# A mixture-of-experts layer that computes only each token's two chosen experts, in sorted tiles of 128 rows

## The chip, the cores and the metric

The kernel runs on one core of a Trainium2 chip. The metric is the device time of one execution in microseconds (us), as the median of several runs. The engines are PE (TensorE, matrix products), DVE (VectorE), ACT (ScalarE), POOL (GpSimd) and SP (SyncE, which here only starts DMAs).

## What is computed

The input x has 16 batches of 128 time steps and 128 features, 2048 tokens in all. Layer 0 is a conditioned projection and a quantised gated feed-forward layer. Layer 1 is a recurrence over time, then a mixture of experts. Cut to what matters here:

```python
# layer 1, cond: a recurrence of 128 steps, on 16 batches at once
xw = x @ Wx + b
h[t] = tanh(xw[t] + h[t-1] @ Wh)
# layer 1, ffn: 8 experts, 128 -> 512 -> 128, two of them per token
logits = h @ router_w.T
values, chosen = top_k(logits, 2);  weight = softmax(values)
y[e] = gelu(h @ w1[e].T + b1[e]) @ w2[e].T + b2[e]
out = x + sum(weight[k] * y[chosen[k]] for k in (0, 1))
```

The reference computes all eight experts for each token and then takes two of them.

## The kernel before, in words

All of it is one program with an instruction stream for each engine. Tokens are in time-major order in the second layer: 16 batches of one time step are 16 neighbouring columns, and 8 steps are one tile of 128 tokens.

**Layer 0** (up to about 107 us) is a chain of products, quantisations by a global maximum, and rounding. DVE and ACT carry most of it. Meanwhile POOL (`split_weights`, L330) scales the expert weights, splits each of 16 chunks into a high and a low float16 part, and SP turns them with a transposing DMA (L275 to L280). The last two chunks are split by ACT (`weight_hi`, L403) and DVE (L701).

**The recurrence.** A step is one float32 matmul of 128x16 on PE (`first_step`, L911, and L985 to L988), which the trace shows as two weight loads and two matmuls, then a Tanh on ACT that writes the state into `h32` (L494, L517). PE's next step waits for that Tanh. The first 16 steps run beside the end of layer 0, the others in slots of the expert layer: `RNN_SLOTS` (L32) says in which of the eight slots of a pair of experts a step is issued.

**The expert layer** is dense. `WIDTHS` (L25) cuts the tokens into five chunks, whose states are complete in turn. `chunks` (L214) goes through the chunks and, in each, through four pairs of experts, three of these as a loop with the pair's number in a register. `pair` exists for PE (L967), ACT (L508) and DVE (L758). One slot is a quarter of one expert for all tokens of the chunk. In it PE makes the hidden product, three matmuls (high x high, low x high, high x low) over up to 512 columns, and the output product `down` (L956) of the slot four earlier, three matmuls of 128 columns for each tile. ACT takes the GELU (L523) and in some slots a second GELU in float16 (L525, `HI_SCALAR`). DVE makes the float16 high part (L789) and the low part (L793), and adds each expert's output, times the token's gate, to the accumulator (`add_gated`, L744). Each expert meets each token, whether it was chosen or not: the gate of one not chosen is zero.

**Routing** is done once for a chunk, in its first slots: logits by PE, top two by DVE (L711 to L742). POOL splits the states into float16 parts (L358), and multiplies the output biases by the gates and sums them (`sum_b2`, L365). SP stores each output tile when its chunk is complete (L282 to L290).

The order on every engine is written out by hand, and each wait is on a semaphore with a known count.

Of the kernel before, what the change touches and what calls it, by code (L numbers as in the profile page):

```python
# [5 lines left out]
F32, F16 = mybir.dt.float32, mybir.dt.float16  # L6
I8, U8 = mybir.dt.int8, mybir.dt.uint8
I16, U16 = mybir.dt.int16, mybir.dt.uint16
ALU = mybir.AluOpType
# [3 lines left out]
P = 128  # L13
# [18 lines left out]
RNN_SLOTS = ((0, 1, 3, 4, 5, 7), range(8), range(8), (0, 1, 2, 4, 5, 6), ())  # L32
RNN_FROM = [FIRST_STEPS + E // 2 * sum(len(n) for n in RNN_SLOTS[:c]) for c in range(CH)]
HI_SCALAR = ((3,), (), (3,), (3,), (0, 1, 3))
TS = P // B
SLOTS = E * NF
WS = 256.0
# [6 lines left out]
W_POOL = 14  # L44
# [4 lines left out]
W_CHUNKS = 2 * E  # L49


def program(nc, x, cond, w_cond, w_gate, w_up, w_down, w_x, w_h, b_h, w_router, w1, b1, w2, b2, out):
    ctx = ExitStack()
    with ctx:
# [6 lines left out]
        def sems(names):  # L61
# [5 lines left out]
        ident = sb("ident", [P, P])  # L67
        ident16 = sb("ident16", [P, P], F16)
# [30 lines left out]
        nat_wy = wyT[:, :, :].rearrange("p b o -> p (b o)").bitcast(F16).rearrange("p (a n) -> p a n", a=4)  # L99
        h32 = q[:, :, :].rearrange("p a n -> p (a n)").bitcast(F32)  # L100
# [6 lines left out]
        rw = sb("rw", [P, E])  # L107
        rw_hi = sb("rw_hi", [P, E], F16)
        rw_lo = sb("rw_lo", [P, E], F16)
        b2_all = sb("b2_all", [P, E, P])  # L110
# [4 lines left out]
        g32 = sig2[:, 0:NF * CT].rearrange("p (f n) -> p f n", f=NF)  # L115
        g_hi, g_lo = (sig2.bitcast(F16)[:, 2 * NF * CT * (i + 1):2 * NF * CT * (i + 2)].rearrange("p (a f n) -> p a f n", a=2, f=NF)
                      for i in range(2))
        h_hi, h_lo = (up2.bitcast(F16)[:, TOK * i:TOK * (i + 1)] for i in range(2))

        b2_prod = gate2[:, 0:E * P].rearrange("p (e n) -> p e n", e=E)  # L120
        b2_sum = gate2[:, E * P:E * P + 2 * CT].rearrange("p (a j n) -> p a j n", a=2, n=P)
        logit = sb("logit", [P, CTILES, E])
        top = sb("top", [P, CTILES, 8])
        topi = sb("topi", [P, CTILES, 8], U16)
        mixd = sb("mixd", [P, 4, CTILES])
        pick = sb("pick", [P, 2, CTILES, E])
        gates = sb("gates", [P, TOK // P, E])
# [3 lines left out]
        ld_cond, ld_gate, ld_up, ld_down, ld_misc, ld_wx, ld_b2 = sems(  # L131
# [20 lines left out]

        ps_rnn = banks[0]
        ps_y = [banks[1], banks[2]]
        ps_logits = banks[3]
        ps_h = banks[4:8]
        ps_pk = banks[7]
        Q_HI_SCALAR = (2, 3)
# [872 lines left out]
```

## Time and profile before

| | us |
|---|---|
| median of 3 runs | 349.01 |
| lowest and highest run | 348.28, 349.47 |
| the profiled execution, whole | 348.25 |
| its span, first to last instruction | 346.5 |
| end of the first 16 steps, start of step 16 | 107.3 |
| DVE busy | 315.1 (91%) |
| PE busy, matmuls | 265.4 (77%) |
| ACT busy | 213.1 (62%) |
| POOL busy | 158.3 (46%) |

The rows further down come from one profiled execution. A time at the start of a row counts from the span's start. PEld is PE's weight load, which runs beside its matmuls; SPq is the queue of DMAs that SP issues. Matmuls overlap, so that the sum of their durations is more than the time in which PE is busy. The arrow in brackets behind a row says how long the engine stood idle before it and who ended that idle time; "issue" means that it waited for nothing that the profile shows.

### The profile page before, as it was taken

Reading aid. Unit: us, or ns where it says so; the run is one execution under the profiler, and the core shown is the slowest. Engines: PE = TensorE matmul, PEld = TensorE weight load, DVE = VectorE, ACT = ScalarE, POOL = GpSimd, SP = SyncE. Lnnn points to the kernel's source line nnn. Section 1 sums busy time; section 2 is a strip of 40 time slices with the busy share of each in tenths; the row PEclk is TensorE's granted clock in tenths of the full one; section 3 lists DMA queues with packets and bytes.
Section 4 is the critical chain, followed back from the end, with each engine's and each line's share of the span. In section 5 each row is a group of like instructions: output and inputs, shape, how many; then the busy total and the mean of one; then the engine's idle time right before and its main releaser. Section 6 shows DMA issues by size and latency. Waiting matters only on the chain.

```text
span 346.5 us, 8439 instructions
## 1 busy us (share of the span) xinstructions
PE 265.4 (77%) x2601; PEld 190.9 (55%) x2601; DVE 315.1 (91%) x648; ACT 213.1 (62%) x427; POOL 158.3 (46%) x198
## 2 busy tenths in 40 slices
PE   5589330006698979997779999888999998776894
PEld 4434230002456867785557776556777666654673
DVE  4899999899996899799999899999889999999985
ACT  6289998160536765775447676555676665574692
POOL 1779994000086156016762109784111676639400
PEclk9989965556998998999999999999999999999999
DMA  7991443000015000000000000000001000001000
GB/s 204 332 282 38 97 86 61 0 0 0 0 33 121 2 0 0 3 2 18 0 0 0 2 23 4 0 0 0 2 0 32 0 1 0 2 3 31 0 2 23
DMA packets 28074, 12.13 MB, mean 35 GB/s; under 512 B 17369, under 2 KB 26898, under 8 KB 28050
## 3 DMA queue, kind: packets, MB, share of 16 engines
q1 hardware_dynamic: 27650, 11.63, 13.0%
q8 instruction: 13, 0.21, 0.2%
q10 hardware_dynamic: 400, 0.20, 0.2%
q14 instruction: 11, 0.09, 0.1%
HBM read 6.58 MB, written 1.05 MB: 22 GB/s over the span
## 4 chain that ended last, share of the span: by engine, by line
PE 39%; DVE 37%; issue 14%; POOL 3%; DVEq 2%; DMA 2%; ACT 2%; SPq 1%; ACTq 0%; POOLq 0%
PE bank L814 38%; DVE big L789 8%; DVE big L793 5%; DVE peak L562 5%; DVE wyT L749 5%; DVE big L658 2%; DVE big L668 2%; DMA x_sb<-in_x 2%; DVE big L641 2%; DVE peak L636 2%; DVE big L674 1%; DVE big L676 1%; POOL wnat L315 1%; POOL big L363 1%; ACT big L523 1%
## 5 line engine op out<-in xcount | busy, mean ns | idle before, releaser
L814 PE MATMUL bank<-wt,big 128*128 (+1 forms) x1536 | 116.3, 221 | 23.3 <-DVE big L793 14.6
L793 DVE TENSOR_TENSOR big<-big 128x384 f16<-128x384 f32 (+2 forms) x160 | 124.8, 787 | 9.5 <-ACT big L525 5.4
L814 PEld LDWEIGHTS bank<-wt,big 128*128 128x128 f16 x1536 | 97.6, 98 | 59.1 <-issue 36.2
L523 ACT ACTIVATE big<-bank,miscT 128x384 f32<-128x384 f32 (+2 forms) x160 | 96.3, 602 | 45.7 <-PE bank L814 41.3
L814 PE MATMUL bank<-big,wt 128*128 128x384 f16 (+2 forms) x480 | 110.3, 339 | 1.4 <-POOL big L363 1.4
L789 DVE CAST big<-big 128x512 f16<-128x512 f32 (+2 forms) x112 | 55.6, 497 | 7.2 <-ACT big L523 6.1
L361 POOL CAST big<-q 128x64 f16<-128x64 f32 x32 | 11.0, 344 | 98.1 <-ACT q L517 98.1
L517 ACT ACTIVATE q<-bank,miscT (+1 forms) x112 | 30.7, 274 | 39.7 <-PE bank L814 38.2
L814 PEld LDWEIGHTS bank<-big,wt 128*128 (+1 forms) x480 | 46.6, 117 | 13.7 <-POOL big L363 1.5
L814 PE MATMUL bank<-q,wxh 128*128 (+1 forms) x254 | 45.2, 254 | 2.1 <-ACT q L494 1.6
L814 PEld LDWEIGHTS bank<-q,wxh 128*128 128x128 f32 x254 | 39.1, 194 | 7.5 <-ACT q L494 3.7
L749 DVE SCALAR_TENSOR_TENSOR wyT<-bank,gates,wyT 128x128 f32<-128x128 f32 x128 | 39.6, 341 | 0.3 <-issue 0.2
L371 POOL TENSOR_TENSOR big<-big 128x512 f32<-128x512 f32 (+1 forms) x32 | 37.3, 1166 | 2.5
L369 POOL TENSOR_TENSOR big<-b_all,gates 128x1024 f32<-128x1024 f32 x16 | 33.7, 2105 | 7.9 <-issue 7.7
L315 POOL TENSOR_SCALAR wnat<-wnat 128x512 f32<-128x512 f32 x14 | 11.5, 818 | 40.1 <-DVE big L674 40.1
L525 ACT ACTIVATE big<-bank,miscT 128x384 f16<-128x384 f32 (+2 forms) x48 | 28.4, 592 | 0.0
L814 PE MATMUL bank<-ident,pk 128*128 128x128 f32 x10 | 2.9, 381 | 26.1 <-DVE pk L550 26.1
L814 PE MATMUL bank<-q,wT_hi 128*128 128x512 f16 x48 | 16.0, 404 | 2.6 <-DVE q L628 2.6
L814 PEld LDWEIGHTS bank<-ident,pk 128*128 128x128 f32 x10 | 2.0, 236 | 28.1 <-DVE pk L550 22.1
L452 ACT ACTIVATE big<-bank 128x512 f32<-128x512 f32 x24 | 14.0, 602 | 2.6 <-PE bank L814 2.0
L363 POOL TENSOR_TENSOR big<-q,big 128x64 f16<-128x64 f32 x32 | 14.2, 445 | 2.6
L814 PE MATMUL bank<-wT_hi 128*128 128x512 f16 x14 | 5.0, 517 | 13.3 <-DVE big L668 13.3
(136 smaller groups left out, 307.6 us busy)
## 6 DMA issues: line engine op xcount, KB each, us to landing
wnat<-in_w SPq DMA_DIRECT2D x8, 512.0 KB, 7.4
x_sb<-in_x SPq DMA_DIRECT2D x4, 256.0 KB, 4.7
out_block<-wyT SPq DMA_DIRECT2D x16, 64.0 KB
b_all<-in_b SPq DMA_DIRECT2D x1, 512.0 KB, 5.5
wn<-in_w_gate ACTq DMA_DIRECT2D x1, 192.0 KB, 5.4
wn<-in_w_up SPq DMA_DIRECT2D x1, 192.0 KB, 6.0
wn<-in_w_down SPq DMA_DIRECT2D x1, 192.0 KB, 6.0
wt<-wyT SPq DMA_TRANSPOSE x8, 3.1
```

The lines of the kernel that those rows point to most:

```text
L315: link(G.tensor_scalar(src, src, WS, 0.0, ALU.mult, ALU.add))
L363: G.tensor_tensor(h_lo[:, at], h32[:, at], h_hi[:, at], ALU.subtract).then_inc(h_lo_done, 1)
L369: link(G.tensor_tensor(b2_prod, b2_all[:, :, :], gate, ALU.mult))
L371: link(G.tensor_tensor(b2_prod[:, 0:n, :], b2_prod[:, 0:n, :], b2_prod[:, n:2 * n, :], ALU.add))
L517: A(h32[:, bass.ds(step * B, B)], ps_rnn[:, bass.ds(rnn_column(c, step), B)], ACT.Tanh, bias=bias_h, scale=1 / WS).then_inc(h32_done, 1)
L523: A(g32[:, f, 0:w], ps_h[f][:, 0:w], ACT.Gelu, bias=bias, scale=1 / WS).then_inc(g32_done, 1)
L525: A(g_hi[:, s // NF, f, 0:w], ps_h[f][:, 0:w], ACT.Gelu, bias=bias, scale=1 / WS).then_inc(g_hi_done, 1)
L562: link(V.tensor_reduce(peak[:, i, n:n + 1], t, X, ALU.max, apply_absolute_value=True))
L749: V.scalar_tensor_tensor(a, ps_y[par][:, P * j:P * (j + 1)], g, a, ALU.mult, ALU.add).then_inc(added, 1)
L789: V.tensor_copy(g_hi[:, par, f, 0:w], g32[:, f, 0:w]).then_inc(hi_v, 1)
L793: V.tensor_tensor(g_lo[:, par, f, 0:w], g32[:, f, 0:w], g_hi[:, par, f, 0:w], ALU.subtract).then_inc(g_lo_done, 1)
L814: return nc.tensor.matmul(o, l, r, start=start, stop=stop, skip_group_check=True)
```

## The change

The expert layer is replaced. The recurrence runs by itself from step 16, and the experts get only the rows that chose them.

- The tokens form two spans (`SPANS`): steps 0 to 71 and 72 to 127. When a span's states are complete, they are turned into rows (`turn_tokens`, a float32 product with the identity and the router's columns beside it), DVE takes the top two and POOL scatters each token's row (128 high parts, 128 low parts) twice to a table in DRAM, sorted by expert, with each expert's rows padded to a multiple of 128.
- The positions come from matmuls with triangular matrices on PE (`rank_tokens`, `place_tiles`) and small operations on DVE (`count_tiles`, `place_tokens`). `owner` holds the expert of each tile. PE and ACT load these numbers into registers, 25 for the first span and 21 for the second, and address weights and biases through them.
- The number of tiles is the largest that can occur: 25 and 21. Every one is computed, also an empty one. SP reads the table back through transposing DMAs (`load_states`).
- Work is planned in quarters (`quarters`). A unit is four quarters: the hidden product of a tile and the output product of the tile two earlier. Two quarters are issued with each step from step 108 on, and after the last step four in each round, 40 rounds.
- DVE copies each tile's output (`take_y`), SP writes it to DRAM (`put_y`), POOL gathers the two rows of each token when the span's last tile is written (`get`), and DVE adds them with their gates (`add_experts`), for the first span in round 161, for the second behind the last round. SP stores the sums.
- b2 and the recurrence's bias enter as one more matmul with the bias rows, in place of `sum_b2` and of ACT's bias.
- Earlier: POOL makes the constants, splits the bias rows, splits 5 weight chunks in layer 0 and 7 behind it (11 and 3 before), DVE splits the last 4 by itself, and ACT none. SP also fills the tables with zeros.

```diff
+SPANS = (1152, 896)
+NT = [(2 * n - E) // P + E for n in SPANS]
+UNITS = [(c, i) for c in range(NS) for i in range(NT[c] + 2)]
+RELEASE = (108, 0)
+LATE = 4
-W_POOL = 14
+W_POOL = 12
+W_EARLY = 5
+TOKENS_AT = [max(TS * (g + 1), FIRST_STEPS + 6 + g) for g in range(NG)]
+RANK_AT = [STEP0[c + 1] + (3 if c < NS - 1 else 2) for c in range(NS)]
+PLACE_AT = [RANK_AT[c] + 2 for c in range(NS)]
+EXPERT_AT = [PLACE_AT[c] + (2 if c < NS - 1 else 1) for c in range(NS)]
+MIX_AT = [min(LAST_Y[0] + 16, END), END]
+LOAD_AT = [FIRST_STEPS, T + 14]
...
@@ sync @@
+            def load_states(c):
+                sp.wait_ge(sent[c], 32 * GT[c])
+                for n in range(LOADS[c]):
+                    at = slice(4 * P * n, min(4 * P * (n + 1), P * NT[c]))
+                    sp.dma_start_transpose(hT[c][:, :, at], xg[c][at, :]).then_inc(ld_ht[c][n], 16)
+            def put_y(c, i, k):
+                sp.wait_ge(y_done, k + 1)
+                sp.dma_start(ygd[c][P * i:P * (i + 1), :], ysb[:, k % 4, :]).then_inc(y_put[k % 4], 16)
...
@@ gpsimd @@
+            def send(c):
+                pool.wait_ge(pos_done, c + 1)
...
+                for g in range(G0[c], G0[c + 1]):
+                    for a in range(2):
+                        G.indirect_dma_start(out=xg[c][:, :], out_offset=bass.IndirectOffsetOnAxis(ap=pos[:, a, g:g + 1], axis=0),
+                                             in_=hrow[:, g, :], in_offset=None).then_inc(sent[c], 16)
+            def get(c):
+                for m in range(4):
+                    pool.wait_ge(y_put[m], puts_before(T0[c + 1], m))
+                for g in range(G0[c], G0[c + 1]):
+                    for a in range(2):
+                        G.indirect_dma_start(out=yg[:, a, g, :], out_offset=None, in_=ygd[c][:, :],
+                                             in_offset=bass.IndirectOffsetOnAxis(ap=pos[:, a, g:g + 1], axis=0)).then_inc(got[g], 16)
...
+            send(0)
+            send(1)
+            get(0)
+            get(1)
@@ scalar @@
+            for r in range(FIRST_STEPS, END):
+                if r < T:
+                    step(r)
+                if r in TOKENS_AT:
+                    take_rows(TOKENS_AT.index(r))
...
+                for q in gelus(r):
...
+                    A(g32[:, k % 2, f, :], ps_h[(NF * k + f) % 3][:, 0:P], ACT.Gelu,
+                      bias=miscT[:, bass.ds(owners[i] * NF + f, 1)], scale=1 / WS).then_inc(g32_done, 1)
@@ vector @@
+            def take_y(k):
+                dve.wait_ge(y_mm, k + 1)
+                if k >= 4:
+                    dve.wait_ge(y_put[k % 4], 16 * (k // 4))
+                V.tensor_copy(ysb[:, k % 4, :], ps_y[k % 2][:, 0:P]).then_inc(y_done, 1)
+            def split_gelu(k):
+                dve.wait_ge(g32_done, NF * (k + 1))
...
+                V.tensor_copy(g_hi[:, k % 3, :, :], g32[:, k % 2, :, :]).then_inc(hi_v, 1)
+                dve.wait_ge(hi_v, k + 1)
+                V.tensor_tensor(g_lo[:, k % 3, :, :], g32[:, k % 2, :, :], g_hi[:, k % 3, :, :],
+                                ALU.subtract).then_inc(g_lo_done, 1)
@@ tensor @@
+            def hidden(c, i, k, f):
+                if f == 0:
+                    pe.wait_ge(ld_ht[c][i // 4], 16)
+                n = NF * k + f
+                if n >= 3:
+                    pe.wait_ge(g32_done, n - 2)
...
+                mm(o, w_hi, hi, True)
+                mm(o, w_hi, lo, False)
+                mm(o, w_lo, hi, False).then_inc(hid_mm, 1)
+            def down(c, i, k, f):
+                o = ps_y[k % 2][:, 0:P]
+                if f == 0:
+                    pe.wait_ge(g_lo_done, k + 1)
...
+                    mm(o, ones[0:LO_ROW + 1, 0:P], rows[:, bass.ds(owners[c][i] * P, P)], True)
...
+            for r in range(FIRST_STEPS, END):
+                if r < T:
+                    if rnn_in(r) is not None:
+                        input_part(rnn_in(r))
+                    step(r)
+                if r in TOKENS_AT:
+                    turn_tokens(TOKENS_AT.index(r))
...
+                for q in range(*PLAN[r]):
+                    if q % NF == 0 and UNITS[q // NF][1] == 0:
...
+                        owners[c] = load_owners(pe, mybir.EngineType.PE, c)
+                    if hidden_of(q):
+                        hidden(*hidden_of(q))
+                    if down_of(q):
+                        down(*down_of(q))
```

The functions that are not quoted are what the list above says of them.

## Rows read from the trace of the kernel before

**Rows 1.** The page: engines' busy time, and shares of the chain of waits.
```profile
PE 265.4 (77%) x2601; PEld 190.9 (55%) x2601; DVE 315.1 (91%) x648; ACT 213.1 (62%) x427; POOL 158.3 (46%) x198
...
PE 39%; DVE 37%; issue 14%; POOL 3%; DVEq 2%; DMA 2%; ACT 2%; SPq 1%; ACTq 0%; POOLq 0%
PE bank L814 38%; DVE big L789 8%; DVE big L793 5%; DVE peak L562 5%; DVE wyT L749 5%; DVE big L658 2%; DVE big L668 2%; DMA x_sb<-in_x 2%; DVE big L641 2%; DVE peak L636 2%; DVE big L674 1%; DVE big L676 1%; POOL wnat L315 1%; POOL big L36
```

**Rows 2.** Windows: us; PE, PEld, DVE, ACT, POOL busy; clock; DMA share; GB/s.
```profile
44.00:66.00 22.00, 2.40 (x13) 2.16 (x12) 21.35 (x21) 14.93 (x13) 11.53 (x10) 0.58 0.24 49
...
107.00:345.00 238.00, 209.75 (x2316) 157.68 (x2313) 218.68 (x500) 148.29 (x326) 105.65 (x127) 0.99 0.03 8
```

**Rows 3.** Timeline of DVE in a chunk of 512: start us, us, operation.
```profile
249.84 0.43 DVE L789 CAST big<-big 128x512 f16<-128x512 f32 x1
...
250.30 0.69 DVE L793 TENSOR_TENSOR big<-big 128x512 f16<-128x512 f32 x1
```

**Rows 4.** Timeline, recurrence steps beside layer 0, and step 16.
```profile
102.48 0.30 PEld L814 LDWEIGHTS bank<-q,wxh 128*128 128x128 f32 x2 [0.26 <-ACT q L494]
...
102.91 0.28 ACT L494 ACTIVATE q<-bank,miscT 128x16 f32<-128x16 f32 x1 [0.48 <-PE bank L814]
...
103.24 0.30 PEld L814 LDWEIGHTS bank<-q,wxh 128*128 128x128 f32 x2 [0.26 <-ACT q L494]
...
107.30 0.30 PEld L814 LDWEIGHTS bank<-q,wxh 128*128 128x128 f32 x2 [0.32 <-ACT wyT L505]
```

**Rows 5.** Timeline, a recurrence step in the expert layer, at the lower clock.
```profile
111.80 0.55 PEld L814 LDWEIGHTS bank<-q,wxh 128*128 128x128 f32 x2
...
112.50 0.27 ACT L517 ACTIVATE q<-bank,miscT 128x16 f32<-128x16 f32 x1
```

**Rows 6.** Windows, the granted clock around the start of the expert layer.
```profile
91.00:103.00 12.00, 9.63 (x59) 5.34 (x60) 11.61 (x14) 5.65 (x14) 6.52 (x7) 1.00 0.13 23
...
107.20:110.60 3.40, 2.00 (x25) 1.72 (x24) 0.97 (x3) 1.23 (x5) 2.62 (x6) 1.00 0.87 197
110.60:114.00 3.40, 3.40 (x26) 3.03 (x25) 2.84 (x15) 2.37 (x7) 0.55 (x2) 0.50 0.04 11
```

**Rows 7.** Timeline of PE's weight loads: steps in chunk 256, the last products.
```profile
120.03 0.30 PEld L814 LDWEIGHTS bank<-q,wxh 128*128 128x128 f32 x2 [0.20 <-issue]
...
121.17 0.30 PEld L814 LDWEIGHTS bank<-q,wxh 128*128 128x128 f32 x2 [0.21 <-issue]
...
339.25 1.15 PEld L814 LDWEIGHTS bank<-wt,big 128*128 128x128 f16 x18
```

**Rows 8.** ACT on 128x128 from a bank (by form); timeline, two DVE adds.
```profile
L429 ACT ACTIVATE c<-bank,nrm 128x128 f32<-128x128 f32 x8 | 2.3, 369 | 1.3 <-PE bank L814 1.1 <-DVE nrm L583 0.2
...
326.46 0.59 DVE L749 SCALAR_TENSOR_TENSOR wyT<-bank,gates,wyT 128x128 f32<-128x128 f32 x2
```

**Rows 9.** Timeline: DVE and POOL at once, twice; DVE with POOL idle.
```profile
124.42 1.90 POOL L369 TENSOR_TENSOR big<-b_all,gates 128x1024 f32<-128x1024 f32 x1
...
124.45 2.15 DVE L793 TENSOR_TENSOR big<-big 128x256 f16<-128x256 f32 x1 [0.47 <-ACT big L525]
...
44.15 1.82 DVE L658 TENSOR_TENSOR big<-big 128x1024 f32<-128x1024 int16 x1
...
59.85 1.23 DVE L658 TENSOR_TENSOR big<-big 128x1024 f32<-128x1024 int16 x1
```

**Rows 10.** Timeline of SP's queue: one transposing DMA, the last three stores.
```profile
99.31 1.23 SPq L280 DMA_TRANSPOSE wt<-wyT  x1
...
342.52 1.90 SPq L289 DMA_DIRECT2D out_block<-wyT  x3
```

**Rows 11.** DMA issues: kind, count, KB each, us from issue to landing.
```profile
wc<-in_w_cond SPq DMA_DIRECT2D x1, 64.0 KB, 1.9
...
wt<-nat SPq DMA_TRANSPOSE x8, 2.7
```

**Rows 12.** The page: the longest group on POOL.
```profile
L369 POOL TENSOR_TENSOR big<-b_all,gates 128x1024 f32<-128x1024 f32 x16 | 33.7, 2105 | 7.9 <-issue 7.7
```

More of the change, by code:

```diff
@@ new lines, in program @@
+        upto = sb("upto", [E, E], F16)
+        seven = sb("seven", [E, 1], F16)
+        tile_no = sb("tile_no", [E, WBLK])
+        count = sb("count", [E, P])
+        tiles = sb("tiles", [E, NS, P], F16)
+        passed = sb("passed", [E, WBLK], F16)
+        owner = sb("owner", [1, NS, WBLK], I32)
+        zeros = sb("zeros", [P, 2 * P], F16)
+        xg = [nc.dram_tensor(f"xg{c}", [NT[c] * P, 2 * P], F16, kind="Internal").ap() for c in range(NS)]
+        ygd = [nc.dram_tensor(f"ygd{c}", [NT[c] * P, P], F32, kind="Internal").ap() for c in range(NS)]
@@ L294, in _ @@
+            for c in range(NS):
+                if MIX_AT[c] == END:
+                    put_out(c)
+            sp.wait_ge(stored, 16 * NG)
         @block.gpsimd
@@ L477, in _ @@
                     take_xT(n + 1)
-            for i in range(W_POOL, W_CHUNKS):
-                weight_hi(i)
             def low_byte(c):
@@ L486, in _, with step @@
                 low_byte(c)
-            act.wait_ge(misc_sb, 1)
-            bias_h = miscT[:, SLOTS:SLOTS + 1]
-            def first_step(r):
+            def step(r):
                 act.wait_ge(rnn_mm, r + 1)
-                at = slice(r * B, (r + 1) * B)
-                A(h32[:, at], ps_rnn[:, at], ACT.Tanh, bias=bias_h, scale=1 / WS).then_inc(h32_done, 1)
-            for r in range(EARLY_STEPS):
-                first_step(r)
+                A(h32[:, r * B:(r + 1) * B], state(r), ACT.Tanh, scale=1 / WS).then_inc(h32_done, 1)
@@ L811, in _ @@
+            for c in range(NS):
+                if MIX_AT[c] == END:
+                    add_experts(c)
         @block.tensor
@@ L929, in _ @@
                     if c >= 2:
[L930 removed]
+                        step((c - 2) * 4 + p)
                     for j in range(NJ):
@@ new lines, in rank_tokens @@
+            def rank_tokens(c):
+                n = GT[c]
+                if c == 0:
+                    pe.wait_ge(routing, 1)
+                pe.wait_ge(row_lo, G0[c + 1])
+                pe.wait_ge(picked_done, c + 1)
+                flat = picked[:, G0[c]:G0[c + 1], :].rearrange("p j e -> p (j e)")
+                mm(ps_route[:, 0:n * E], below[:, :], flat, True)
+                for d in range(1, n):
+                    mm(ps_route[:, d * E:n * E], ones[:, 0:P], flat[:, 0:(n - d) * E], False)
+                for j in range(n):
+                    last = mm(ps_route[0:E, P:2 * P], picked[:, G0[c] + j, :], ones[:, 0:P], False)
+                last.then_inc(rank_mm, 1)
```

610 lines of the change are left out of this document (308 added, 302 removed).

## The prediction

> **What bounds the kernel now.** I read the page's engine shares and chain of waits first, then windows by stage, then timelines for single prices. DVE is busy for 91% of the span and PE for 77%, and the chain that ended last is spread over PE 39%, DVE 37% and issue 14% [rows 1]: two engines take turns at the end of each wait. From 107 to 345 us, the expert layer, DVE works 219 of 238 us and PE's matmuls cover 210 [rows 2]. So the dense layer is full on two engines, and the recurrence of 112 more steps runs inside it for nothing. That is what the change turns around: it takes away most of the dense work, and the recurrence loses its cover.
>
> In work: 16 tiles by 8 experts were 128 tile passes, now there are 46. The price is that most of the 46 can only start when states exist, are sorted and are fetched back, and that they run in pieces of 128 columns. I add up the new end in five stretches, against the profiled span of 346.5 us, which the profiled execution's 348.25 us exceeds by 1.75; that is 0.8 below the median of 349.01. A measurement here tells about 0.3% from no change, that is 1 us.
>
> **A. To step 16, now at 107.3 us [rows 4].** POOL does 5 weight chunks early instead of 11. Beside its work the same DVE pass took 1.82 us, alone 1.23 [rows 9]; three or four of the six passes of that stage win something, some 2 us. The bias rows on POOL (three operations over 1152 elements, estimate 5 us by 2.1 us for 1024 [rows 12]) push the third weight matrix by about 1 us; step 16 no longer waits for its input product, about 1 us. Splitting moved from ACT to DVE, the constants and the zero fill lie beside waits or in the recurrence, where DVE and POOL are idle: nothing, and if that cover went, four chunks on DVE cost some 5 us. Sum -2, between -4 and +3: **105.3**.
>
> **B. Steps 16 to 107, alone.** At the full clock a step takes 0.76: weight load at 102.48, Tanh at 102.91, next weight load at 103.24 [rows 4]. At half clock the Tanh starts 0.70 behind the weight load (111.80 to 112.50) instead of 0.43, takes 0.27 [rows 5], and 0.05 later PE may go on: 1.02. Which clock is granted? With PE busy 9.6 of 12 us it stayed at 1.00; the stretch with 2.0 of 3.4 us was followed by one at 0.50, the lower level of 1.2 GHz [rows 6]. A lone step keeps PE less busy than either, so I take 1.02: 92 x 1.02 = 93.8. Added on PE: 13 turnings of a tile, of which Tanh and copy hide most, 0.25 each (0.1 to 0.6); 18 small matmuls for the positions at twice the 0.064 of [rows 7], 2.3, and two short waits; three input products at some 1.2 each behind what the Tanh hides. Together 9.3 (5 to 14). 103: **208.3**.
>
> The Trainium skill, "TensorE: Matmul & The Clock Gate", section "Why this matters for your kernels", asks only that no long idle gap lies between matmuls, and the gaps inside a step are well below it. By that rule the clock would stay up; the last two windows of [rows 6] disagree, with no idle time of that length either. It is a rival below.
>
> **C. Steps 108 to 127, with two quarters each.** A hidden product has three banks. ACT takes the GELUs of one step's quarters behind the next step's Tanh, so the second quarter's hidden product waits for: step to Tanh 0.43, Tanh 0.27, GELU 0.37 (128 columns from a bank, [rows 8]), hand-over 0.05, then its own 0.5, in all 1.6 to 1.65 (bounds 1.3 if PE alone counts, 2.0 at the lower clock). The 0.5 is two groups of three 128-column matmuls. Streaming with fixed addresses they take 1.15/18 = 0.064 each [rows 7]; in the slots whose addresses come from registers, 11 matmuls take 121.17 - 120.03 = 1.14, 0.104 each, with 0.2 of "issue" before the step [rows 7]. So a group is 0.19 to 0.31; I take the middle, 0.25, since every group now has two register addresses and no long columns behind which they hide. 20 x 1.65 = 33. Register loads: 25 on PE and then 25 on ACT, in series since each holds up the other. No row shows one; the bounds are a register operation hidden in the stream (0.03) and a DMA's landing (1.9, [rows 11]); nearest is the issue gap of 0.2: 10 us (2 to 25). 43: **251.3**. Are the rows fetched in time? Positions are done near 173 us; 18 scatters at 1.23 (below), landing 2, transposing 1.2 and 2.7 [rows 10, 11] give 201, so there are 7 us to spare.
>
> **D. The 40 rounds.** They hold 144 hidden and 152 output groups, 296 x 0.25 = 74, and 38 bias matmuls, 4. DVE needs per round 0.30 for the copy ([rows 8]), 0.43 and 0.69 for the split [rows 3], with hand-overs 1.6, against PE's 1.95: hidden, and an excess of 18 adds of 0.30 in round 161 takes 2 units of slack, which there are. If PE ran at 0.19 per group, both would be level. Then 21 loads, side by side on both engines, 4; routing of the second span, 2. 84 (60 to 105): **335.3**.
>
> **E. Behind the last matmul.** Nothing covers this. Copy 0.4, store issue 0.6 [rows 10], landing 1.9 [rows 11]; then 14 gathers in POOL's queue. Their price is in no row: at least 0.63, a plain DMA's issue on SP, at most 2.1, POOL's longest operation [rows 12]; I take 1.23, the issue of a transposing DMA [rows 10], as the nearest that also makes many small pieces: 17.2. Landing 2, two adds 0.6, seven stores at 0.63, 4.4, landing 2. 29 (20 to 43): **364.3**, plus 1.75: **366 us**. In short, 238 us of dense layer become 103 + 43 + 84 + 29 = 259.
>
> **Rivals.**
> 1. *Forecast*, 366, chance 0.52: recurrence at half clock, tiles at 0.25 a group, bare tail.
> 2. *The register addresses hide* (faster, 0.24). For: with a backlog PE dispatches ahead, and the fixed stream ran at 0.064. C becomes 20 x 1.5 + 2.5 = 32.5, D 296 x 0.19 + 38 x 0.064 + 3 = 62: 334 us. The side turns where PE's group costs about 0.22 and the loads half of mine. Against: 0.104 in [rows 7].
> 3. *POOL's indirect DMAs starve* (0.15). POOL and DVE shut each other out: a DVE pass next to POOL's took 2.15 us [rows 9] and ended just behind it. Beside DVE's splits at 2.1 each: scatters come 10 late for step 108, the second span's 11 for its first tile, the tail grows by 12: about 395; at 1.7 about 380. The skill's "SBUF — State Buffer", section "SBUF: two separate sides", says that a DVE pass on the shared port keeps POOL from writing DMA descriptors; the trace shows the lock between the engines, no run here the DMAs. The tail has no DVE work beside it, which speaks against the last 12.
> 4. *The clock stays up* in B (0.05): 92 x 0.26 = 24 less, 342.
> 5. *The end is set by something that the sum leaves out* (0.04), such as a queue on SP, where output stores stand behind the six transposing loads of the second span: their wait for the scatters stops the output copies after four tiles; 5 to 15 more, 376.
>
> That less work is done is sure: the number of tiles is fixed in the program.
>
> **Numbers.** Faster: rivals 2 and 4 and little of 1's own spread, less what of 2 falls short: 0.27. Within 0.3%: 0.05. Slower: 0.68. The range goes from the upper half of rival 2 to the milder form of 3: 340 to 388; the forecast's own is 352 to 380.
>
> **What would show it.** Right: a granted clock of 0.5 from step 16 to 107 and a period near 1.02; a first expert matmul near 215 us; rounds of 2 us with PE as the engine that others wait for; a stretch of some 29 us at the end with PE idle and POOL issuing. Wrong: steps of 0.76; rounds below 1.7 or set by DVE; gathers far from 1.23; a wait of PE on the transposed rows at step 108 or at the change of spans; register loads of a microsecond.

## The result, and the profile after

The changed kernel takes 360.99 us, the median of four runs from 358.39 to 362.66; the kernel before, beside it, 348.65. The ratio is 1.034, with a 95% interval of 1.027 to 1.042: slower, by 12.3 us. The forecast was 366. The profiled execution, the slowest of the four, took 362.66 us whole, with a span of 360.9. Ratios here and below leave out a run that lies over 1.5% above the fastest of its kernel, which concerns one run each of two kernels below, the one with fixed experts (median 337.52 us, 335.97 without that run) and the one with two fillers (351.62 and 351.53).

The page of the profile after, the lines that answer to [rows 1], and the granted clock in 40 slices of 9 us:

```profile
PE 249.6 (69%) x1746; PEld 186.4 (52%) x1746; DVE 188.8 (52%) x422; ACT 151.0 (42%) x414; POOL 112.3 (31%) x136
...
PEclk9969765559995555555555555579999899989555
...
PE 46%; DVE 28%; POOL 8%; issue 6%; ACT 5%; DMA 4%; SPq 1%; ACTq 1%; POOLq 0%; DVEq 0%
PE bank L914 46%; DVE peak L655 5%; POOL xg L478 5%; DVE peak L729 4%; POOL wnat L487 3%; ACT q L583 2%; DVE big L761 2%; DVE big L751 2%; DMA wn<-in_w_up 2%; DVE big L798 1%; DVE big L734 1%; DVE wyT L882 1%; DVE big L796 1%; DMA big<-xg 1
```

DVE fell from 91% to 52% and PE from 77% to 69%: no engine is full any more. The work became less, and what took its place is waiting and a slow clock: from the 13th slice to the 26th PE is granted half of its 2.4 GHz, that is its lower level of 1.2 GHz.

Windows of the profile after, by stretch; the columns are those of [rows 2] (the lone recurrence, the steps with experts, two pieces of the rounds, the tail):

```profile
108.00:192.00 84.00, 61.72 (x232) 50.72 (x231) 15.28 (x71) 19.16 (x101) 28.12 (x30) 0.51 0.21 45
196.00:234.00 38.00, 34.32 (x257) 28.74 (x258) 13.13 (x33) 14.11 (x56) 0.00 (x0) 0.50 0.21 46
236.00:266.00 30.00, 29.80 (x321) 22.46 (x319) 18.53 (x56) 18.35 (x52) 13.29 (x14) 0.95 0.18 57
283.00:312.00 29.00, 28.65 (x303) 21.09 (x302) 16.45 (x36) 17.66 (x49) 17.74 (x18) 1.00 0.27 70
335.00:361.00 26.00, 0.00 (x0) 0.00 (x0) 4.30 (x14) 0.00 (x0) 13.21 (x14) 0.50 0.20 53
```

The first two stretches are at 0.50, but for the first microsecond, the rounds nearly at 1.00. The last has no PE work at all. In the five stretches of the prediction, each from the trace:

| stretch | forecast | measured |
|---|---|---|
| A, Tanh of step 16 | 105.7 | 106.0 |
| B, step 16 to 108 | 103 | 88.3 |
| C, step 108 to 127 | 43 | 39.6 |
| D, step 127 to the last matmul | 84 | 98.1 |
| E, behind the last matmul | 29 | 28.8 |

(A is the forecast's 105.3 plus 0.43 from weight load to Tanh.) The forecast's span of 364.3 is only 3 us over the profile's 360.9, although B and C were 18 us too long in it and D 14 us too short: that the errors nearly cancel is luck.

**The lone recurrence.** Timeline of the profile after, two steps at the full clock, then one at half:

```profile
107.66 0.30 PEld L914 LDWEIGHTS bank<-q,wxh 128*128 128x128 f32 x2 [0.37 <-ACT q L583]
...
108.09 0.18 ACT L583 ACTIVATE q<-bank 128x16 f32<-128x16 f32 x1 [0.48 <-PE bank L914]
...
108.33 0.30 PEld L914 LDWEIGHTS bank<-q,wxh 128*128 128x128 f32 x2 [0.37 <-ACT q L583]
...
192.01 0.50 PEld L914 LDWEIGHTS bank<-q,wxh 128*128 128x128 f32 x2 [0.38 <-ACT q L583]
...
192.66 0.18 ACT L583 ACTIVATE q<-bank 128x16 f32<-128x16 f32 x1 [0.70 <-PE bank L914]
192.89 0.50 PEld L914 LDWEIGHTS bank<-q,wxh 128*128 128x128 f32 x2 [0.38 <-ACT q L583]
```

At the full clock the period is 0.67 (107.66 to 108.33), at half 0.88 (192.01 to 192.89), against 0.76 and the forecast's 1.02. The Tanh takes 0.18 instead of the 0.28 in [rows 4].

**The start of the experts.** Timeline of PE's matmuls and of ACT:

```profile
196.27 0.82 PE L914 MATMUL bank<-big,wt 128*128 128x128 f16 x6 [1.89 <-DMA big<-xg]
...
197.47 0.18 ACT L583 ACTIVATE q<-bank 128x16 f32<-128x16 f32 x1 [2.88 <-PE bank L914]
199.55 0.62 ACT L623 ACTIVATE big<-bank,miscT 128x128 f32<-128x128 f32 x2 [1.89 <-issue]
```

PE stands still for 2 us before its first expert matmul, ACT for 1.89 before its first GELU. In the trace both hold one load instruction there, of 2.06 us on PE from 193.99 and of 1.92 on ACT from 197.48: all 25 registers in one instruction. The profile names a DMA of the rows as releaser on PE, whose transposing DMAs started at 192.65; either alone would account for the wait, as the run with fixed experts shows below.

**The rounds.** Timeline of PE's weight loads (PEld) and of DVE's output copies, one round:

```profile
301.13 0.22 PEld L914 LDWEIGHTS bank<-big,wt 128*128 x3
...
301.38 0.24 PEld L914 LDWEIGHTS bank<-wt,big 128*128 128x128 f16 x3
...
301.65 0.22 PEld L914 LDWEIGHTS bank<-big,wt 128*128 x3
...
301.90 0.24 PEld L914 LDWEIGHTS bank<-wt,big 128*128 128x128 f16 x3
...
300.46 0.29 DVE L859 COPY big<-bank 128x128 f32<-128x128 f32 x1 [0.94 <-PE bank L914]
...
302.85 0.29 DVE L859 COPY big<-bank 128x128 f32<-128x128 f32 x1 [0.80 <-PE bank L914]
```

A group of three matmuls starts every 0.25 us at best (301.13, 301.38, then 301.65, 301.90), quarters have small gaps between them, and a round is 2.39 here, 2.46 on average. The records of PE's own queue, which hold register operations too, say why (start in us, ns, instruction; one output group, and the register operation of the next):

```
301.806    46 FUSED_REGOPS
301.902    96 LDWEIGHTS
301.930    46 FUSED_REGOPS
302.026    96 LDWEIGHTS
302.041    99 LDWEIGHTS
302.054    46 FUSED_REGOPS
```

From one register operation to the next, with a matmul between them, it is 0.124 us, 0.096 of it from the operation to the weight load behind it. Each group has two distinct addresses, the high and the low weights, so 0.248. Without register operations the three matmuls need 0.17, as the run with fixed experts shows below.

**The tail.** Timeline of POOL, DVE and SP behind the last matmul:

```profile
335.04 0.94 POOL L487 DMA_INDIRECT wnat<-ygd,pos  x1 [27.52 <-DMA ygd<-big]
336.29 0.94 POOL L487 DMA_INDIRECT wnat<-ygd,pos  x1 [0.31 <-issue]
...
353.85 0.35 DVE L878 SCALAR_TENSOR_TENSOR wyT<-wnat,mixd,wyT 128x128 f32<-128x128 f32 x1 [2.21 <-DMA wnat<-ygd,pos]
354.12 1.92 DVE L882 SCALAR_TENSOR_TENSOR wyT<-wnat,mixd,wyT 128x128 f32<-128x128 f32 x7
354.49 4.51 SPq L373 DMA_DIRECT2D out_block<-wyT  x7
```

A gather every 1.25 us, 14 of them, with PE and ACT idle and only DVE's seven first adds beside them; then seven second adds, with seven stores issued behind them.

### The profile page after: what moved, and what is told of

It reads as the page before. It is cut to its first block, busy times and chain, and to the rows that moved or that the text cites. A ratio compares the mean times of both kernels' runs of the same rounds, so it can differ in the third digit from the quotient of the medians.

```text
span 360.9 us, 5896 instructions
## 1 busy us (share of the span) xinstructions
PE 249.6 (69%) x1746; PEld 186.4 (52%) x1746; DVE 188.8 (52%) x422; ACT 151.0 (42%) x414; POOL 112.3 (31%) x136
## 4 chain that ended last, share of the span: by engine, by line
PE 46%; DVE 28%; POOL 8%; issue 6%; ACT 5%; DMA 4%; SPq 1%; ACTq 1%; POOLq 0%; DVEq 0%
PE bank L914 46%; DVE peak L655 5%; POOL xg L478 5%; DVE peak L729 4%; POOL wnat L487 3%; ACT q L583 2%; DVE big L761 2%; DVE big L751 2%; DMA wn<-in_w_up 2%; DVE big L798 1%; DVE big L734 1%; DVE wyT L882 1%; DVE big L796 1%; DMA big<-xg 1%; DVE x_sb L781 1%
## 5 line engine op out<-in xcount | busy, mean ns | idle before, releaser
L914 PE MATMUL bank<-q,wxh 128*128 128x16 f32 x254 | 68.0, 347 | 21.9 <-ACT q L583 21.8
L623 ACT ACTIVATE big<-bank,miscT 128x128 f32<-128x128 f32 x184 | 64.9, 366 | 42.4 <-PE bank L914 33.4
L914 PE MATMUL bank<-big,wt 128*128 128x128 f16 x552 | 72.8, 249 | 7.4 <-ACT big L623 3.2
L914 PE MATMUL bank<-wt,big 128*128 x552 | 76.7, 245 | 0.2
L478 POOL DMA_INDIRECT xg<-big,pos x32 | 31.1, 970 | 115.9 <-issue 58.5
L583 ACT ACTIVATE q<-bank 128x16 f32<-128x16 f32 x128 | 23.4, 183 | 87.1 <-PE bank L914 87.1
L914 PEld LDWEIGHTS bank<-big,wt 128*128 x552 | 46.1, 112 | 18.9 <-issue 12.3
L914 PEld LDWEIGHTS bank<-wt,big 128*128 128x128 f16 x552 | 42.8, 106 | 11.0 <-issue 0.6
L487 POOL DMA_INDIRECT wnat<-ygd,pos x32 | 31.0, 967 | 55.0 <-DMA ygd<-big 45.8
L868 DVE TENSOR_TENSOR big<-big 128x512 f16<-128x512 f32 x46 | 32.1, 697 | 1.6
L914 PEld LDWEIGHTS bank<-ident_r,pk 128*128 128x128 f32 x10 | 2.0, 237 | 25.6 <-DVE pk L643 19.3
```

The source lines that it names most:

```text
L478: G.indirect_dma_start(out=xg[c][:, :], out_offset=bass.IndirectOffsetOnAxis(ap=pos[:, a, g:g + 1], axis=0), in_=hrow[:, g, :], in_offset= ...
L487: G.indirect_dma_start(out=yg[:, a, g, :], out_offset=None, in_=ygd[c][:, :], in_offset=bass.IndirectOffsetOnAxis(ap=pos[:, a, g:g + 1], a ...
L583: A(h32[:, r * B:(r + 1) * B], state(r), ACT.Tanh, scale=1 / WS).then_inc(h32_done, 1)
L623: A(g32[:, k % 2, f, :], ps_h[(NF * k + f) % 3][:, 0:P], ACT.Gelu, bias=miscT[:, bass.ds(owners[i] * NF + f, 1)], scale=1 / WS).then_inc(g ...
L868: V.tensor_tensor(g_lo[:, k % 3, :, :], g32[:, k % 2, :, :], g_hi[:, k % 3, :, :], ALU.subtract).then_inc(g_lo_done, 1)
L914: return nc.tensor.matmul(o, l, r, start=start, stop=stop, skip_group_check=True)
```

## The experiments

Each edit is to the changed kernel unless the text says otherwise. Durations inside a run come from its profile; times of kernels are medians of their runs, beside the kernel before at 347.94 to 348.68 us.

### Is it the clock, and is it PE's idling that lowers it?

```diff
 step(r)
+if 17 <= r < 108:
+    for _ in range(times):
+        mm(banks[7][:, 0:cols], wT_hi[:, 0, :], wT_hi[:, 0:cols // 128, :], True)
```

It ran with one filler of 256 columns, one of 512, and two of 512:

> The changed kernel with one more float16 matmul of 128x256, into a bank that is idle then, behind each recurrence step from 17 to 107; its result is used by nothing. Theory (the lone recurrence is slow because PE, busy for too little of each step, is granted 0.5): if the filler is enough the granted clock stays near 1.0 in this stretch, a step takes 0.67 us as in steps 17 to 19 instead of 0.88, 88 steps win 18 us, and if the stretch with two quarters a step also starts at the full clock, its 20 steps win up to 0.4 each: 335 to 343 us in all. Rival (the filler is too small for the clock, or the clock is set by something other than PE's own work): granted clock 0.5 from 109 us on, steps of 0.88 to 0.95, 361 to 367 us.

> The same filler with 512 columns instead of 256. At the full clock its matmul and weight load should take about 0.27 us, as long as PE idles in a step now, so a step would be 0.67 to 0.75. Theory: clock 1.0 in the lone recurrence, 337 to 346 us. If the clock rises here and not with 256 columns, the amount of PE work decides. Rival (nothing raises the clock): at half clock the filler takes over 0.45 us and stands in front of the next step, steps of about 1.1, 378 to 385 us.

> The changed kernel (360.99 us) with two filler matmuls of 512 columns behind each recurrence step from 17 to 107, where one of 256 and one of 512 left the granted clock at 0.5. Theory A (the clock follows how many columns PE streams, not whether it idles): the clock comes back to 1.0 in the lone recurrence, where a step then takes 0.40 for its own matmuls and 0.47 for the fillers, 0.87 to 0.95, about what it is now; the first steps with experts start at the full clock and are shorter: 355 to 365 us. Theory B (nothing in the lone recurrence raises it): the fillers at half clock take 0.9 and stand in front of the next step, 1.35 to 1.5 a step, 90 steps by 0.5 to 0.6: 405 to 418 us.

Measured: 362.64, 367.05 and 351.62 us. Windows of 130 to 150 us, in the changed kernel and the three with fillers, in this order:

```profile
130.00:150.00 20.00, 14.57 (x52) 12.43 (x52) 1.85 (x12) 4.93 (x26) 0.00 (x0) 0.50 0.00 1
```
```profile
130.00:150.00 20.00, 18.80 (x75) 12.94 (x75) 1.84 (x12) 4.95 (x26) 0.00 (x0) 0.50 0.00 0
```
```profile
130.00:150.00 20.00, 20.00 (x74) 13.06 (x72) 1.85 (x12) 4.77 (x25) 0.00 (x0) 0.50 0.00 0
```
```profile
130.00:150.00 20.00, 20.00 (x122) 10.77 (x122) 2.22 (x16) 5.66 (x31) 0.00 (x0) 1.00 0.00 1
```

With one filler of 512 columns PE is covered for 20.00 of 20 us, and the clock stays at 0.50. With two it is 1.00. So filling PE's idle time was not what counted, and the theory as the first run put it fell. Of the third run's two theories A held as far as the clock: more work on PE brought it back. Whether the columns are what counts, or the number of matmuls or weight loads, these runs don't separate, since the third doubles them all. The sizes missed too. With one filler of 512 a step is still 0.88, and only those with a turning or other work beside them grow (1.12 for 0.88), so the total was 367.05 and not 378 to 385. Most steps with two fillers take 0.67, not 0.87 to 0.95, the same as a bare one at the full clock, since the fillers fit under the Tanh; the total lies below the 355 to 365 expected. Steps 16 to 108 fell from 88.3 to 73.0 us. The kernel is 1.011 (1.004 to 1.017) of the kernel before. The Trainium skill, "TensorE: Matmul & The Clock Gate", section "Why this matters for your kernels", asks that PE be kept busy, without long idle gaps; by that rule the second run should have had the full clock, and its window says otherwise.

The medians differ by 9.4 us only, the two profiled executions by 14.8 (one is the fastest of its kernel, the other the slowest). What stands against the gain is the start of the experts. PE's timeline in the run with two fillers, the first expert matmul:

```profile
187.14 0.82 PE L914 MATMUL bank<-big,wt 128*128 128x128 f16 x6 [7.90 <-DMA big<-xg]
```

PE now waits 7.90 us for the rows, since POOL's 18 scatters, 1.26 each, do not get faster with the clock: the cover of 7 us that the forecast counted was there because the recurrence was slow. From the Tanh of step 108 to that of step 109 it is 9.1 us instead of 3.1. In this profile the steps with experts win it back, since the clock is at 1.0 again from 198 us on: C is 39.9 us, against 39.6. The other runs have no profile, so where they lose more stays open.

### Do register addresses set the rounds?

```diff
-owners = load_owners(...)          # on PE and on ACT
+owners = [i % E for i in range(NT[c])]
```

> The changed kernel in which tile i uses expert i modulo 8, a constant: PE and ACT load no registers and no address comes from one. It leaves out the choice of the tile's expert; all other work stays. Theory of the prediction (a register address in each group costs PE about 0.06 us and shows as issue time): the 40 rounds fall from 2.4 us by 0.5 (8 groups by 0.06), 20 us, and the two pairs of register loads of 1.5 to 2.1 us go, 4 to 7 us: 333 to 340 us. Rival (the rounds are set by the weight loads of 128x128 matmuls, or by the hand-over between PE, ACT and DVE): only the loads go, 354 to 358 us.

Measured: 337.52 us (334.20 to 339.48), 23.5 less, within the theory's range. Timeline of this run's PE weight loads and of DVE's output copies:

```profile
240.37 0.29 DVE L859 COPY big<-bank 128x128 f32<-128x128 f32 x1 [0.22 <-PE bank L914]
...
240.71 0.21 PEld L914 LDWEIGHTS bank<-big,wt 128*128 128x128 f16 x3
...
240.88 0.21 PEld L914 LDWEIGHTS bank<-wt,big 128*128 128x128 f16 x3
...
241.05 0.21 PEld L914 LDWEIGHTS bank<-big,wt 128*128 128x128 f16 x3
...
241.97 0.29 DVE L859 COPY big<-bank 128x128 f32<-128x128 f32 x1
```

Without registers a group starts every 0.17 us instead of 0.25, and a round is 1.60 instead of 2.46: 0.86 for eight groups, 0.107 each, of which 0.08 is seen between groups and the rest between quarters. The theory of the prediction held; its 0.06 a group was too small. That the total came out in the range is partly luck, since two things that were not counted nearly cancel. D fell from 98.1 to 81.6 us only, where 37 full rounds by 0.86 would be 32: DVE's adds in the middle (9.5 us between two of its output copies, 6.0 in the changed kernel) and the change of spans took most of the rest. At the latter the faster PE met rows that were not there:

```profile
258.93 3.19 PE L914 MATMUL bank<-big,wt 128*128 128x128 f16 x27 [4.82 <-DMA big<-xg]
```

And the wait of 3.0 us at the first expert step stayed without any register load on PE (3.02 between the Tanhs of steps 108 and 109, 3.06 before): the transposed rows were not there earlier. Of the loads before the rounds only ACT's cost anything, some 2 us in the next step (3.46 against 1.38). C fell by 12.0 us in this profile, from 39.6 to 27.6, which the expectation did not count: these 2, and the steps behind them, which take 1.23 us with the clock at 1.0 (window of 208 to 223 us in this run) where the changed kernel took 1.87 to 1.96 at 0.50:

```profile
208.00:223.00 15.00, 13.84 (x177) 11.21 (x176) 8.97 (x22) 8.52 (x38) 0.00 (x0) 1.00 0.09 27
```

This run takes the registers from ACT's GELUs as well. The next one changes PE's output products alone:

```diff
 o = ps_y[k % 2][:, 0:2 * P]  (as p, 2, n)
-mm(o, hi, w_hi, False)
-mm(o, hi, w_lo, False)
-last = mm(o, lo, w_hi, False)
+w_both = w_pair(owners[c][i], f)   # high and low weights, one address
+mm(o, hi, w_both, f == 0)
+last = mm(o, lo, w_both, False)
...
-V.tensor_copy(ysb[...], ps_y[k % 2][:, 0:P])
+V.tensor_reduce(ysb[...], both halves, X, ALU.add)
```

> The changed kernel with the output product in two matmuls of 128x256, on the high and low weights side by side under one address, into two halves of a bank that DVE adds in the copy, in place of three of 128x128 under two addresses. It adds the product low x low, and PE makes 598 register operations instead of 782. Theory (each distinct register address costs PE's queue about 0.124 us, as the trace and the fixed-expert run say together): an output group falls from 0.30 to about 0.22 us, where its 512 columns limit it, so 152 groups behind the recurrence win 12 us; beside the recurrence at half clock the extra columns cost 2 to 3: 350 to 354 us. Rival (the columns or the semaphores set the group, not the addresses): 152 by 0.05 more, 366 to 370 us.

Measured: 347.31 us, 13.7 less, below the 350 to 354 expected, and 0.997 of the kernel before (0.994 to 0.9998). DVE's sums of two neighbouring rounds in this run:

```profile
251.32 0.42 DVE L864 TENSOR_REDUCE big<-bank 128x128 f32<-128x256 f32 x1 [0.44 <-PE bank L920]
...
253.33 0.42 DVE L864 TENSOR_REDUCE big<-bank 128x128 f32<-128x256 f32 x1 [0.52 <-PE bank L920]
```

A round is 2.01 here and 1.93 in the plain ones, so 0.13 less for each of the four output groups, close to the 0.124 of one register operation. D is 87.3 us, 10.8 less. In the profile C is 6.2 us less as well, since the clock rose in it, and step 16 comes 2.5 later.

### Steps with experts

```diff
-RELEASE = (108, 0)
+RELEASE = (128, 0)
```

> The changed kernel in which no expert work is issued before step 128: the recurrence runs alone to its end, and the rounds with four quarters become 50 instead of 40. Theory of the prediction (expert work beside the recurrence saves time, since a step and two quarters take 1.65 us and the same apart 1.02 + 1.0): 7 us more, 367 to 370. Rival (at half clock, interleaving saves nothing: the 20 steps with two quarters take 40 us, alone they take 20 by 0.88 = 18 and the ten rounds 10 by 2.4 = 24): within 2 us of 361.

Measured: 364.81 us, 3.8 more. From step 108 to the last matmul it is 138.6 us instead of 137.7; the rest is mostly layer 0, which the edit does not touch and which took 3.4 us more in this profile. The total lies between the theory and the rival, and neither range held; in the stretch itself the rival is right, for interleaving gains 0.9 us there with the clock at 0.50. That it could gain more shows in the windows of 204 to 228 us, of the changed kernel and of the one in which only the order of the last adds differs (below), so that both run the same instructions here:

```profile
204.00:228.00 24.00, 23.61 (x178) 19.73 (x178) 9.30 (x26) 9.51 (x38) 0.00 (x0) 0.50 0.05 15
```
```profile
204.00:228.00 24.00, 21.69 (x216) 16.71 (x216) 10.90 (x29) 11.49 (x47) 0.00 (x0) 0.91 0.06 18
```

In the second the clock rose to 1.0 from step 113 on and a step with two quarters takes 1.49 to 1.54 instead of 1.87 to 1.96, and C is 34.0 us instead of 39.6. That would also explain the spread of the changed kernel's own four runs, of which only the slowest has a profile: their mean clocks are 0.713, 0.718, 0.742 and 0.740 at 362.7, 362.3, 359.7 and 358.4 us.

### The Tanh

```diff
-A(h32[...], state(r), ACT.Tanh, scale=1 / WS)
+A(h32[...], state(r), ACT.Tanh, bias=zeros[:, 0:2].bitcast(F32), scale=1 / WS)
```

> The changed kernel with a bias tile of zeros in each Tanh of the recurrence, as the kernel before had one (the bias of the recurrence). Result unchanged. Theory (the prediction's step of 1.02 us was too long because the Tanh without a bias tile takes 0.18 us instead of 0.27): each Tanh takes 0.27, a lone step 0.97 instead of 0.88, and the 112 steps alone and beside experts give 8 to 10 us: 369 to 371 us. Rival (the Tanh is shorter for another reason, such as no other work on ACT): 0.18 us as now, 360 to 362 us.

Measured: 371.63 us, 10.6 more, just above the 369 to 371 expected. The page's group of this Tanh:

```profile
L583 ACT ACTIVATE q<-bank,zeros 128x16 f32<-128x16 f32 x128 | 35.0, 274 | 87.1 <-PE bank L915 86.4
```

274 ns against 183 without the tile, and a lone step of 0.97 against 0.88. B is 95.0 us instead of 88.3, C the same (39.7), so the steps with experts do not hang on the Tanh, against the expectation, which counted all 112; of the 9.0 us between the two profiled executions the rest lies before step 16 (1.6) and in the rounds (0.7). The gain that the forecast missed was in the change itself: with the bias moved to a matmul, each lone step lost 0.09.

### The tail and the adds

```diff
 for g in range(G0[c], G0[c + 1]):
     first add of tile g
-for g in range(G0[c], G0[c + 1]):
     dve.wait_ge(mixed, g + 1)
     second add of tile g
```

> The changed kernel in which DVE adds a tile's second expert right behind its first, instead of the first ones of all tiles and then the second ones. Theory (the end is in series: last gather landed, one add, seven adds beside seven store issues of 0.64, landing): the first six output tiles are stored while POOL still gathers, and behind the last gather two adds, one store issue and one landing are left: 3 to 4 us less, 357 to 358. Rival (the stores are limited elsewhere, or the adds in the middle of the rounds get longer by as much, since each second add now waits for its first): 360 to 362 us.

Measured: 357.03 us, 4.0 less, and its tail is 25.6 us instead of 28.8. The 3.2 are the theory's; its rounds took 1.2 more, and how often the clock rises in C moves the total too, as above. In the changed kernel the 18 adds of the first span stand in one piece, in round 160 (the text ahead and the prediction say 161). Timeline of DVE, and the PE matmul behind them:

```profile
313.94 2.44 DVE L878 SCALAR_TENSOR_TENSOR wyT<-wnat,mixd,wyT 128x128 f32<-128x128 f32 x9
...
316.30 2.44 DVE L882 SCALAR_TENSOR_TENSOR wyT<-wnat,mixd,wyT 128x128 f32<-128x128 f32 x9
...
320.14 0.22 PE L914 MATMUL bank<-rows,ones 33*128 x1 [2.25 <-DVE big L868]
```

4.9 us of DVE and 2.25 of PE, where the forecast had given two units of slack and no cost. The next version has the output product and the order of adds from above, and spreads these adds:

```diff
-if r == MIX_AT[c]: add_experts(c)
+if c == 0 and r >= MIX_AT[c]: add_experts(c, mix_tiles(r))
```

`mix_tiles(r)` is two tiles a round, and SP stores them one round later.

> The two changes of the output product and of the order of adds together, and the 18 adds of the first span spread over five rounds from 160 on, two tiles a round, with their stores one round later, instead of in one piece that holds up DVE for 4.9 us and PE for 2.3. If the three gains add up: 8 to 11, 3 to 4 and 2 us, 344 to 348 us, level with or a little below the kernel before. If the wait for the transposed rows at the change of spans takes back what PE wins before it (in the fixed-expert run it grew from 6.2 to 9.0 us): 348 to 352 us.

Measured: 339.87 us (338.73 to 343.13), 0.977 of the kernel before (0.970 to 0.984): faster than the changed kernel and than the one before, and below the 344 to 348 expected; whether by more than 2% than the one before, the interval leaves open. It is 21.1 us less than the changed kernel, of which the parts alone had shown 13.7 and 4.0; against the run with the output product alone the rounds are 4.5 us shorter (82.8 for 87.3), where 2 were expected of the spread adds.

### Two waits whose removal gained nothing

The first is on PE, in steps 22 to 24 of the changed kernel (timeline of DVE's split of a weight chunk, its top two, and PE's next turning):

```profile
109.98 1.52 DVE L798 SCALAR_TENSOR_TENSOR big<-wnat,big 128x512 f16<-128x512 f32 x1
...
113.66 0.16 DVE L807 FIND_INDEX8 topi<-top,bank 128x8 uint16<-128x8 f32 x1
...
113.87 0.82 PE L914 MATMUL bank<-ident_r,q 128*128 128x136 f32 x2 [2.66 <-DVE topi L807]
```

The prediction had put DVE's four weight chunks beside idle time. They stood in front of the first tile's top two, and PE waited 2.66 us, with the recurrence behind it: 3.7 us between two Tanhs. This is the cover that it had priced at 5 us if it went.

```diff
-TOKENS_AT = [max(TS * (g + 1), FIRST_STEPS + 6 + g) for g in range(NG)]
+TOKENS_AT = [max(TS * (g + 1), FIRST_STEPS + 12 + g) for g in range(NG)]
...
-RANK_AT = [STEP0[c + 1] + (3 if c < NS - 1 else 2) for c in range(NS)]
-PLACE_AT = [RANK_AT[c] + 2 for c in range(NS)]
+RANK_AT = [STEP0[c + 1] + (3 if c < NS - 1 else 1) for c in range(NS)]
+PLACE_AT = [RANK_AT[c] + (2 if c < NS - 1 else 1) for c in range(NS)]
-LOAD_AT = [FIRST_STEPS, T + 14]
+LOAD_AT = [FIRST_STEPS, T + 12]
```

The first edit, the second, and both:

> The version with the 256-column output product and the reordered and spread adds (339.87 us), with the tokens' turnings begun at step 28 instead of 22. Theory (the 3.7 us between the Tanhs of steps 23 and 24 and the 1.9 behind it come from PE waiting for DVE's top two of tile 0, which stand behind DVE's splits of four weight chunks): that pair of steps takes 0.88 each or little more, 3 to 4 us less: 336 to 337 us. Rival (the turnings bring their own wait wherever they are): 339 to 341 us.

> The same version (339.87 us), with the second span's positions computed in rounds 129 to 131 instead of 130 to 133, and its rows read back from round 140 instead of 142. Theory (the 5.7 us step between two splits at the change of spans, against 1.93 in a plain round, is PE waiting for rows that were scattered late, because the small position products on PE stand behind four quarters of expert work each): positions 4 to 5 us earlier, the wait for the transposed rows gone, 2 to 4 us less: 336 to 338 us. Rival (the change of spans is slow because of the two register loads of 1.5 us in series and the other waits): 339 to 340 us.

> Both of these together on the same version. If they are independent: 5 to 8 us less, 332 to 335 us, 0.955 to 0.965 of the kernel before. If one covers the other: 336 to 338.

Measured: 339.58, 342.41 and 340.02 us, on the version with 339.87; to the kernel before 0.973, 0.982 and 0.976, with intervals of about 0.006 to each side. None is a gain, and all three theories missed in the total; the first total lies in its rival's range, the other two in none. In the first the 2.66 us are gone, but two turnings one step apart now each wait 0.81 us for DVE, so the stretch to step 108 won 1.8 us; C and the rounds gave it back (0.8 and 0.9 us), the clock rising two steps later. In the second the rows came earlier, and the wait at the change of spans only changed its name. Timeline of that run (PE's first matmul of the second span, SP's next output stores, DVE's next sum):

```profile
266.94 0.85 PE L923 MATMUL bank<-big,wt 128*128 128x128 f16 x9 [1.18 <-issue]
267.12 2.77 SPq L376 DMA_DIRECT2D ygd<-big  x5
...
268.99 0.42 DVE L868 TENSOR_REDUCE big<-bank 128x128 f32<-128x256 f32 x1 [4.34 <-DMA ygd<-big]
```

PE's wait of 1.18 is "issue", the register load of 1.63 us, where the version had 1.17 for the rows; and the transposing DMAs, two rounds earlier in SP's queue, now hold up the stores of outputs, so that DVE waits 4.34 us for a buffer. From 268 to 274 us the clock is 0.57 in this run and 1.00 in the version it started from. So the rival of the second expectation was right that the register load is the next wait. The 2.5 us more in the total lie here: between two of DVE's output sums, five apart and on either side of the change of spans (262.83 to 278.30 us, against 262.44 to 275.55), the profile is 2.4 us longer, and its other differences cancel. How DVE's wait and the lower clock share the 2.4 isn't separated. It stays open whether two fillers of 512 columns a step would shorten the version with 339.87 too: that wasn't tried.

## Why the prediction was right or wrong, point by point

- **The total, 366.** 5 us over the median of 360.99, by terms that were off by 18 us one way and 14 the other. The mechanism was right in its main parts (the recurrence alone at half clock, register addresses as the price of a group, a bare tail); the nearness of the number is partly luck.
- **A, 105.3.** Right. Step 16's Tanh came at 106.0; over the profiles of all runs it lay between 106.1 and 109.5, so the 2 us of gain are within what this stretch varies by. The three operations on the bias rows took 5.0 us (1.14, 1.20 and 2.68), as forecast, though the price given for them, 2.1 us for 1024 elements, makes 7: luck.
- **B, 103.** The clock was right: granted 0.5 from 109 us on, and the rival with a clock that stays up fell. The step was mis-sized, 1.02 for 0.88. The term that failed is "takes 0.27, and 0.05 later PE may go on": the Tanh took 0.18, since the bias that the change moves to PE costs 0.09 of it (274 ns against 183), and from weight load to Tanh it was 0.65, not 0.70, from Tanh to weight load 0.23, not 0.32. 92 steps by 0.14 are 13 of the 15 us. The additions of 9.3 came to some 8, but for another reason: single turnings cost nothing, and the first two 3.8 through DVE's queue.
- **C, 43.** Right by two errors. The register loads were not 10 us but one instruction of about 2 us on each engine, and PE's lay beside the wait for the rows. The 1.65 for a step took the full clock, but the clock stayed at half, the bound of 2.0: 1.87 to 1.96 with both products. At the full clock it is 1.5.
- **Rows in time.** Positions at 168 us instead of 173, scatters of 1.26 each; the first transposed rows at about 196, with nothing to spare, since the recurrence was 15 us faster than forecast.
- **D, 84.** The right cause, mis-sized: "a group is 0.19 to 0.31; I take the middle, 0.25". It was 0.295 (a round of 2.46 less the 0.1 that the forecast gives a bias matmul, by eight), at the upper end, and 0.19 without registers. 296 by 0.045 are 13 of the 14 us. The middle of two bounds was no evidence: the two bounds measured two cases, and the change had the dearer one in every group. The 0.104 behind the upper bound is a mean over unlike matmuls (two of float32, three of 256 columns, six of 128); the six of 128 columns with the gap behind them (120.55 to 121.17 in the trace before) give 0.103 each, so the bound stands. "Hidden, there is slack" for the 18 adds was wrong by 2.3 us. At the change of spans two splits lie 6.2 us apart, against 2.46 in a round; PE's longest wait in it is 1.67, the load of 21 registers.
- **E, 29.** Right: 28.8, gathers of 1.25 for the 1.23 taken from the transposing DMA. That they agree is luck: the one is issued by POOL and the other by SP, and no row tied their prices.
- **Rival 2** (the register addresses hide, 334) fell; the run without them took 337.5, but that is no proof of its sum: B was 88 us and not 103, C 28 and not 32.5, and D 82 and not 62, and these errors cancel.
- **Rival 3** (indirect DMAs starve; its three delays of 10, 11 and 12 add up to 399, not 395) fell: the 32 scatters, 14 of them beside DVE's splits, have a median of 958 ns, a longest of 1193. The rule of the Trainium skill, "SBUF — State Buffer", section "SBUF: two separate sides", that was weighed there was not seen at work with these DVE operations.
- **Rival 4** (the clock stays up in B) fell, as said under B.
- **Rival 5** did not set the end, but its place mattered: SP's queue is where the earlier transposing DMAs turned into a wait of DVE.
- **Its own signs.** Two of the signs of being wrong did occur: PE waited for the transposed rows at step 108, and a register load took over a microsecond, 2.06. Of the signs of being right, the half clock and the tail came as said; the period was 0.88 and not 1.02, the first expert matmul came at 196 us and not 215, and a round took 2.46 and not 2.

Where the expected gain went: 238 us of dense layer became 88 + 40 + 98 + 29 = 255 (the first from step 16). The work on DVE fell from 219 to about 90 us in this part, but 88 us of recurrence lost its cover and 29 us of sorting and fetching had none.

## What to carry to other kernels

Price an address from a register as an instruction of its own in the engine's queue: count distinct addresses, not matmuls, and put two operands under one address where a wider matmul allows it. When a change takes work away, look first at what that work had covered, and at the clock that it had kept up. A fetch that only just hides behind a slow stretch is the next wait when that stretch is made faster.

## What the runs showed of the hardware beyond what was expected

- PE, covered for 20.00 of 20 us by the profile, whose ends of matmuls are modelled, was granted 0.50 with one filler of 512 columns in each step, and 1.00 with two. Being busy in the profile's sense and being granted the full clock are two things.
- The same instructions ran once with the clock back at 1.0 in the steps with experts and once without, 34.0 and 39.6 us. These 5.6 us are more than the 4.3 between the fastest and the slowest run of the changed kernel.
- A load of 25 registers is one instruction of 1.90 to 2.14 us, one of 21 takes 1.48 to 1.66. The Trainium skill, "Runtime: NRT & Kernel Launch", section "Instruction fetch mechanics", gives about 200 ns a register, for loads that the same page describes as coming from HBM; by that figure 25 would be an estimate of 5 us. Here they come from SBUF, and the trace decides for 2.
- A bias tile makes a Tanh of 128x16 0.09 us longer, 274 ns against 183.
- An indirect DMA of 128 rows of 512 bytes costs POOL's queue 1.25 to 1.26 us in either direction, 0.95 busy and 0.30 to the next.
